# A masked attention block in fp32: a third Q/K product moved ahead of the output projection, and each residual added before the input is split

## The reference

```python
q = heads(x @ Wq + bq); k = heads(x @ Wk + bk); v = heads(x @ Wv + bv)
scores = einsum('bhqd,bhkd->bhqk', q, k) / sqrt(64)
bias   = where(adj, 0.0, -9e15)[:, None]
probs  = softmax(scores + bias, axis=-1)
ctx    = einsum('bhqk,bhkd->bhqd', probs, v)      # heads joined again: (128, 128, 384)
out    = layernorm(x + ctx @ Wf + bf)
```

## Time and profile before

| | before |
|---|---|
| median of 3 runs | 1088.62 us (1088.13 to 1091.04) |
| the profiled execution, its own time | 1088.34 us |
| its span, first to last instruction | 1086.6 us |
| mean granted TensorE clock | 0.996 |
| PE busy | 1031.7 us, 95% |
| DVE busy | 741.7 us, 68% |
| POOL busy | 635.0 us, 58% |
| ACT busy | 593.1 us, 55% |

### The profile page before, as it was taken

How to read it: one execution, slowest core, us unless ns; L and a number is a source line. 1 busy time by engine, 2 the same in 40 slices (tenths; PEclk the granted TensorE clock), 3 DMA queues, 4 the chain that set the end, 5 groups by cost and what they waited for, 6 DMA issues and landing times.

```text
span 1086.6 us, 26751 instructions
## 1 busy us (share of the span) xinstructions
PE 1031.7 (95%) x7161; PEld 903.0 (83%) x7161; DVE 741.7 (68%) x2823; ACT 593.1 (55%) x2119; POOL 635.0 (58%) x652
## 2 busy tenths in 40 slices
PE   8999999999999999999999999999999999999985
PEld 7888888888888888888888888888888888888874
DVE  3677767766776777677677677767766776776665
ACT  4664654654655655645546546556556456465452
POOL 1355565565566656656655655655566566556566
PEclk9999999999999999999999999999999999999998
DMA  7256656666665656656656656656566666564444
GB/s 196 69 159 177 173 165 183 183 178 175 176 168 167 176 167 171 163 172 162 176 164 170 164 169 171 170 166 175 166 170 172 169 166 167 173 165 148 140 138 133
DMA packets 338970, 179.63 MB, mean 165 GB/s; under 512 B 222592, under 2 KB 322560, under 8 KB 338944
## 3 DMA queue, kind: packets, MB, share of 16 engines
q1 hardware_dynamic: 338544, 178.74, 59.5%
q10 hardware_dynamic: 400, 0.59, 0.1%
HBM read 103.75 MB, written 75.50 MB: 165 GB/s over the span
## 4 chain that ended last, share of the span: by engine, by line
PE 33%; ACT 31%; issue 18%; DVE 15%; DMA 1%; POOL 1%; ACTq 1%; DVEq 1%; SPq 0%; POOLq 0%
ACT probs L623 22%; PE scores_ps L354 9%; PE cov_ps L368 8%; DVE y_sb L532 5%; PE cov_ps L338 5%; ACT kT L641 5%; PE cov_ps L340 4%; PE cov_ps L339 4%; DVE xT_lo L489 4%; DVE stats L535 3%; ACT xT_hi L610 2%; ACT qT L641 2%; PE qk_ps L338 1%; PE qk_ps L339 1%; PE qk_ps L340 1%
## 5 line engine op out<-in xcount | busy, mean ns | idle before, releaser
L623 ACT ACTIVATE probs<-s_mask,neg_max 128x128 f32<-128x128 f32 x768 | 297.4, 390 | 5.5 <-DVE neg_max L506 5.5
L500 DVE CUSTOM_DVE_ANT_0 s_mask<-scores_ps,mask_bias 128x128 f32<-128x128 f32 x768 | 172.5, 287 | 134.4 <-PE scores_ps L354 126.2
L714 POOL TENSOR_TENSOR probs<-probs,inv_sum 128x768 f32<-128x768 f32 x128 | 188.9, 1476 | 80.0 <-DVE inv_sum L519 80.0
L709 POOL TENSOR_SCALAR y_sb<-y_sb,mean_var,rstd 128x384 f32<-128x384 f32 x127 | 209.8, 1652 | 23.4 <-POOL rstd L703 23.4
L512 DVE STREAM_TRANSPOSE p_turned<-probs 128x768 f32<-128x768 f32 x128 | 125.2, 978 | 116.2 <-POOL probs L714 116.1
L338 PE MATMUL cov_ps<-wv_hi,xT_hi 128*128 128x384 f32 x384 | 133.5, 348 | 35.1 <-DVE y_sb L532 33.5
L703 POOL TENSOR_TENSOR rstd<-var_eps,minus_half 128x1 f32<-128x1 f32 x128 | 71.9, 562 | 157.1 <-DVE var_eps L541 153.7
L632 ACT COPY v_sb<-cov_ps 128x384 f32<-128x384 f32 x128 | 61.3, 479 | 176.2 <-PE cov_ps L340 176.2
L641 ACT ACTIVATE qT<-qk_ps,bq_col 128x512 f32<-128x512 f32 x96 | 65.5, 682 | 154.4 <-PE qk_ps L340 154.4
L623 ACT ACTIVATION_READ_ACCUMULATOR probs<-s_mask,neg_max 128x1 f32 x768 | 144.8, 189 | 0.0
L690 POOL TENSOR_SCALAR mask_bias<-adj_u 128x128 f32<-128x128 uint8 x128 | 38.1, 298 | 172.2 <-issue 86.8
(11 more groups left out here) (57 smaller groups left out, 2090.8 us busy)
## 6 DMA issues: line engine op xcount, KB each, us to landing
p_out<-p_turned SPq DMA_DIRECT2D x128, 384.0 KB, 2.3
pT<-p_out SPq DMA_DIRECT2D x512, 96.0 KB, 2.2
x_in<-in_x SPq DMA_DIRECT2D x128, 192.0 KB, 2.6
out<-y_sb SPq DMA_DIRECT2D x128, 192.0 KB, 2.2
x_blocks<-in_x SPq DMA_DIRECT2D x360, 64.0 KB, 2.3
adj_u<-in_adj SPq DMA_DIRECT2D x32, 64.0 KB, 2.2
y_sb<-in_L_gnn_Wq ACTq DMA_DIRECT2D x1, 576.0 KB, 4.7
s_mask<-in_L_gnn_Wk SPq DMA_DIRECT2D x1, 576.0 KB, 6.1
```

The lines of the kernel that those rows point to most:

```text
L500: last = nc.vector.tensor_tensor_reduce(out=s_mask[:, e, h, :], in0=scores_ps[:, score_cols(e, h)], in1=mask_bias[:, e, :], scale=SCALE, s ...
L623: last = nc.scalar.activation(probs[:, e, h, :], s_mask[:, e, h, :], ACT.Exp, bias=neg_max[:, e, h:h + 1], scale=1.0, accum_out=row_sum[:, ...
L709: nc.gpsimd.tensor_scalar(y_sb[:, y, :], y_sb[:, y, :], mean_var[:, e, 0:1], rstd[:, e, 0:1], ALU.subtract, ALU.mult).then_inc(y_ready, 1)
L714: nc.gpsimd.tensor_tensor(probs[:, e, :, :], probs[:, e, :, :], inv_sum[:, e, :].unsqueeze(2).broadcast_to([P, HEADS, SEQ]), ALU.mult).the ...
```

## The change

On TensorE all three Q/K jobs of a step run in one go, after the context products; the output products follow, then V directly behind them. In the steps before step 0 the third job thereby also runs ahead of the transposes and of the bias product. On VectorE residual_and_stats is cut in two: add_residual(e) (line 532) and find_stats(e) (lines 534 to 547). The new order behind invert_sums(1) is add_residual(0), turn_blocks(1), add_residual(1), split_x(0), split_x(1), find_stats(0), find_stats(1). ScalarE's, GpSimd's and SyncE's orders stay, and no wait is added or taken out.

```diff
@@ tensor, step
-                for j in jobs[:2]:
+                for j in jobs:
                     qk_product(i, c, j)
...
                 if real(p - LAG, PAIRS):
                     for e in range(2):
                         out_product(c, p, e)
-                for j in jobs[2:]:
-                    qk_product(i, c, j)
                 if real(p + AHEAD, PAIRS):
@@ vector
-            def residual_and_stats(i, c, e, n):
+            def add_residual(i, c, e, n):
...
                 nc.vector.tensor_tensor(y_sb[:, y, :], cov_ps[e][:, 0:HID], x_bias[:, at % X_RING, :], ALU.add
                                         ).then_inc(y_added, 1)
+
+            def find_stats(c, e, n):
+                y = (2 * (c - LAG) + e) % Y_RING
                 past(dve, y_added, n)
                 nc.vector.bn_stats(stats[:, e, :], y_sb[:, y, :]).then_inc(y_stats, 1)
@@ vector, step
                     invert_sums(1, 2 * p + 1)
+                if real(p - LAG, PAIRS):
+                    add_residual(i, c, 0, 2 * (p - LAG))
+                if real(p, PAIRS):
+                    turn_blocks(i, c, 1, 2 * p + 1)
+                if real(p - LAG, PAIRS):
+                    add_residual(i, c, 1, 2 * (p - LAG) + 1)
                 if real(p + X_AHEAD, PAIRS):
                     for e in range(2):
                         split_x(c, e, 2 * (p + X_AHEAD) + e)
...
                 if real(p - LAG, PAIRS):
-                    residual_and_stats(i, c, 0, 2 * (p - LAG))
-                if real(p, PAIRS):
-                    turn_blocks(i, c, 1, 2 * p + 1)
-                if real(p - LAG, PAIRS):
-                    residual_and_stats(i, c, 1, 2 * (p - LAG) + 1)
+                    for e in range(2):
+                        find_stats(c, e, 2 * (p - LAG) + e)
```

## The result

| | before | changed |
|---|---|---|
| median | 1089.66 us (4 runs, 1088.13 to 1091.04) | 1043.96 us (4 runs, 1042.55 to 1045.41) |
| ratio, 95% interval | | 0.958, 0.956 to 0.960 |
| the profiled execution, its own time | 1088.34 us | 1045.41 us |
| its span | 1086.6 us | 1043.6 us |

The profiled execution of the changed kernel is the slowest of its four, so its 42.9 us less is a little under the 45.7 us between the medians.

A forecast was written before the change was run, and what follows sets the result against it. TensorE bounds the kernel, with one wait a step for VectorE's residual: 58 x (16.50 - 15.68) = 47.6 us saved, 1.4 + 4 lost, -42.2 on 1088.34 gives 1046.1, or 1046.5 for the median; range 1041 to 1066.

The forecast's parts named there:

- What bounds: TensorE, nearly always busy, waits once a step for VectorE's residual(1) before V(1): 0.72 us, 0.82 with a slow first matmul.
- TensorE's floor from steps 60 and 61: Steps 60 and 61, where VectorE has no input to turn and split, take 15.68 us, against 16.50 before them.
- where shapes change over nothing else is seen in the starts: On TensorE, the changed order has the same matmuls, so reordering them leaves the 15.68 us floor as it is.
- New waits on TensorE: Job c, V(0) and V(1) meet no new wait; margins 0.5 to 0.7 us for job c, 0.7 for V(1).
- The splits: VectorE's pair of split_x takes 0.95 us in its new place, clear of GpSimd's normalise_probs, instead of 1.81.
- Rival 2: The splits keep 1.81 us, so the VectorE and GpSimd ring sets 16.1 us a step: 1070 us, chance 0.14.
- neg_max: VectorE's neg_max(0), at 2.57 to 2.74 of a step, stays ahead of GpSimd's second line 709, at 2.7, keeping 0.17 us.
- Rival 1: GpSimd's line 709 holds neg_max(0) up to 1.6 us, every other step, 15.83 on the mean: 1055 us, chance 0.18.
- Rival 3: Line 709 comes ahead of neg_max(0) in every step, about 16.6 us each: slower, 1098 us, chance 0.04.
- SyncE: Its store of y waits until 4.5 for GpSimd, costing nothing, as the queue has over 1 us to spare each step.
- Start: At step -2 job c runs ahead of the transposes, delaying TensorE's first V: 1.4 us lost, bounds 0 and 2.1.
- End: In the last steps sequence 0's statistics stand behind turn_blocks(1) and residual(1): 4 us lost, bounds 0 and 6.

The follow-up runs named there:

- experiment 1: Two kernels against the one before: VectorE's new order with TensorE's old one, 1043.30 us; TensorE's new order with VectorE's old one, 1094.23 us.
- experiment 2: Kernel before with only the statistics moved behind both residuals, 1043.22 us; changed kernel with statistics back right behind each residual, 1065.30 us.
- experiment 4: Changed kernel with both statistics ahead of both splits, so that the splits meet GpSimd's scaling of y: 1047.33 us.
- experiment 3: Changed kernel with the statistics of sequence 0 between the two splits, bringing GpSimd's scaling of y ahead of neg_max(0): 1046.34 us.
- new SyncE order: Changed kernel with the loads of x moved into SyncE's waits between storing and loading the probabilities: 1043.17 us.

## Why the prediction was right

The forecast, 1046.5 us in 1041 to 1066, against 1043.96: right in its mechanism, and within 0.3% partly because errors cancelled.

- **What bounds.** Right. V(1) behind residual(1) was the one wait of each step, and it cost 0.82 us. Its cure is VectorE's order alone (experiments 1 and 2).
- **TensorE's floor from steps 60 and 61**, 15.68. Right for the old order: experiment 1 has 15.68 in every step. In the new order a step takes 15.61. The term "where shapes change over nothing else is seen in the starts" was mis-sized: job c takes 2.04 us behind job b (535.41 to 537.45) and 2.09 between output and V. That explains 0.05 of the 0.07 us. Over 58 steps the floor was 3.5 us too high (58 x 15.68 = 909.4 against 905.9), nearly all of the middle's error of 3.8.
- **New waits on TensorE.** None came. Job c behind job a's copy, V(0), V(1) all held their margins; residual(1) started at 12.59 of the step, 12.66 forecast.
- **The splits.** 0.93 us measured, 0.95 forecast; median of line 489 (now 487) 550 ns. Rival 2 fell with it. The reason given, that the first of the pair waits for all of GpSimd's instruction, holds for the case of the earlier trace rows alone (experiment 4).
- **neg_max.** The position, 2.7, was right to 0.1 us. That GpSimd's scaling of y can hold neg_max was right as well, but not by up to 1.6 us: the longest hold is 0.3 us, it needs a start in two stretches of the scaling, and ScalarE's slack absorbs it (experiment 3). Rival 1 had 0.18 of the chances on one row, and that row was of another GpSimd instruction. Rival 3, built on the same long hold, falls too. The Trainium skill ("SBUF — State Buffer", "Who interferes with whom") says that the loser of the port pair waits for all of the other's instruction; neg_max beside the mask bias agrees with it (0.32 us), neg_max beside the scaling of y (0.17 us in the midst of it, and at most 0.49) and the splits beside it (1.34 and 2.02 us) do not.
- **SyncE.** This step failed: "the queue has over 1 us to spare in each step". It has none: a cycle takes 15.60 us on the mean against steps of 15.61, and the lag never closes. The time to spare was that of a queue which had caught up, in steps of 16.50. While it is behind, its loads go out 2.6 us after the issue of a store, in both kernels (steps 6 to 14 of the one before, steps 6 to 57 of the changed one); once it waited for VectorE, from step 15 of the kernel before, 2.0 us. Why the wait is longer then no run shows. The queue goes into the steady part already late (7.5 us by step 2). It cost only 0.3 us in the profiled execution of the changed kernel (one step over 15.75; 905.9 us for the 58 steps against 905.6 with the new SyncE order), so the time was still right.
- **Start.** 1.4 forecast, 4.1 measured. Three parts: the first Q product itself came 0.9 us later (10.10 against 9.24), before anything of the change, in a start that waits for the first loads of x and varies by as much between the kernels (9.1 to 10.1); V waited 1.7 us longer than that; and behind this gap the granted clock fell to its lower level, 1.2 GHz, for a while, which the prediction left out. Windows of 2 us, clock third from the right:

```profile
20.00:22.00 2.00, 1.50 (x8) 1.50 (x9) 0.45 (x1) 0.00 (x0) 0.60 (x2) 0.94 0.76 119
22.00:24.00 2.00, 2.00 (x8) 2.00 (x7) 0.00 (x0) 0.48 (x1) 0.00 (x0) 0.50 0.64 101
24.00:26.00 2.00, 2.00 (x9) 1.88 (x8) 0.00 (x0) 0.48 (x1) 0.00 (x0) 0.71 0.56 88
```

  V starts at 20.50 and job 3 at 25.31, 4.81 us; the same matmuls took 3.25 before (17.92 to 21.17, at full clock). The 4.1 is one profile's: the kernels with the same TensorE start need 35.3 to 38.0 us up to step 0, 2.1 to 4.8 more than before. The lowest, TensorE's order alone, kept its full clock.
- **End.** 4 forecast, 4.4 measured; with the old order there, TensorE's new order and the new queue 42.1 us, the 42.3 of before.

The errors, -3.8 us in the middle and +3.0 outside it, partly cancelled; that part of the closeness is luck.

## What to carry to other kernels

Look for steps in the trace of the kernel before that leave out just the suspected work: they measure the floor without building anything. When two engines meet once a step, find what the other one waits for and check that it comes in time; one microsecond of work moved out of its way was enough here, and the larger reordering added little. Before a rival is called refuted by two instructions that overlapped unharmed, look at which distances they were at. After a gain on the bound, add up the cycle of the queues too, with their waits for landings, and take it from a stretch in which the queue is behind, since one that waits for an engine hides it. A queue that no longer waits for any engine is the next bound.

## What the runs showed of the hardware that I had not expected

GpSimd's tensor_scalar over 384 elements with two scalars read from SBUF (1.65 us) holds VectorE's small tensor_scalar only if that starts 0.20 to 0.51 or 1.19 to 1.49 us into it, and by 0.3 us at most. GpSimd's mask bias (0.30 us, uint8 in) and, in the one row there is, add_bias (1.0 us) hold it to their end. Beside GpSimd's tensor_scalar, two-tensor subtractions on VectorE and the GpSimd instruction both grow by 0.35 us. A gap of 3.3 us on TensorE in the start was followed by some 3 to 4 us at half clock in the changed kernel, one of 2.7 us was too (statistics between the splits), one of 1.55 us, in the kernel before, was not; but one of 3.3 us in TensorE's order alone was not either, so the length of the gap alone does not decide it. And a queue that stores 384 KB to DRAM and loads it back issues those loads 2.6 us behind the store's issue while it is behind, and 2.0 us once it has caught up, in one and the same kernel.
